# Experts: the order of SyncE's store of X, the unit in which the routing weights are turned, and ACT's order at entry

## The reference, cut to what matters

```
xn = layernorm(x) * gamma + beta
abel_out = gelu(xn @ abel_w + abel_b)
logits = xn @ gate_w + gate_b                       # 8 experts
topw, topi = top_k(logits, 2); topw = softmax(topw)
w_dense = sum(one_hot(topi) * topw)                  # token x expert weights
h = gelu(xn @ ew1[e] + eb1[e])                       # every expert, on every token
eo = h @ ew2[e] + eb2[e]
moe = sum_e eo * w_dense[e], then three rotations
gate = sigmoid(concat(abel_out, moe) @ gc_w + gc_b)
x = x + 0.5 * (layernorm(x) + abel_out * (1 - gate) + moe * gate)
```

## Time and profile before

| | |
|---|---|
| median of 3 runs | 1024.81 us (1024.4 to 1026.99) |
| the profiled execution | 1027.39 us, of which the span of its instructions is 1025.7 us |
| mean granted TensorE clock, as a share of full speed | 0.931 |
| busy: PE, DVE, ACT, POOL | 84%, 71%, 63%, 59% of the span |
| stage 4 | from about 307 to 544 us of the span |
| stage 6 | from about 775 us to the end |

### The profile page before, as it was taken

The page is one execution under the profiler, slowest core; times in us unless marked ns, Lnnn a source line. Parts: engine busy times, 40 slices in busy tenths (PEclk is TensorE's granted clock), DMA queues, the critical chain, the costliest instruction groups (busy, mean ns, idle before and its releaser), DMA issues.

```text
span 1025.7 us, 14084 instructions
## 1 busy us (share of the span) xinstructions
PE 859.0 (84%) x3830; PEld 459.1 (45%) x3830; DVE 725.1 (71%) x1549; ACT 648.1 (63%) x1169; POOL 604.2 (59%) x611
## 2 busy tenths in 40 slices
PE   7889777678966999999994888888866998889997
PEld 6744333373423444444442455555534444444443
DVE  6945479964555788888872477777784878877774
ACT  3177499957745888888763343333324878777874
POOL 2164776566468776666673354444457757555664
PEclk9989799969986999999997899999986999999999
DMA  8000000000002222222200000000002221122220
GB/s 209 11 2 0 0 1 1 0 1 2 0 0 83 83 84 83 82 83 82 82 1 1 0 1 1 1 1 1 1 0 83 84 73 46 68 93 93 93 93 21
DMA packets 27406, 42.10 MB, mean 41 GB/s; under 512 B 5320, under 2 KB 19036, under 8 KB 27356
## 3 DMA queue, kind: packets, MB, share of 16 engines
q1 hardware_dynamic: 27356, 41.52, 12.2%
HBM read 39.15 MB, written 2.36 MB: 40 GB/s over the span
## 4 chain that ended last, share of the span: by engine, by line
PE 28%; issue 26%; POOL 21%; DVE 16%; ACT 5%; DMA 1%; SPq 1%; POOLq 1%; DVEq 0%; ACTq 0%
POOL arena L786 10%; PE bank L1476 5%; PE bank L1478 5%; PE bank L1477 5%; POOL arena L806 5%; POOL arena L750 4%; PE bank L1700 3%; DVE arena L1317 1%; ACT bank L993 1%; DVE stats L1166 1%; PE bank L1670 1%; PE bank L1707 1%; PE bank L1559 1%; DMA arena<-wrows 1%; ACT arena L989 1%
## 5 line engine op out<-in xcount | busy, mean ns | idle before, releaser
L786 POOL TENSOR_TENSOR arena<-arena 128x512 f16<-128x512 f32 x256 | 294.5, 1162 | 141.7 <-ACT arena L989 139.9
L1317 DVE TENSOR_TENSOR arena<-bank,arena 128x512 f32<-128x512 f32 x256 | 173.6, 685 | 89.7 <-ACT bank L993 48.5
L989 ACT ACTIVATE arena<-arena 128x512 f16<-128x512 f32 x256 | 161.3, 630 | 81.5 <-DVE arena L1317 81.0
L993 ACT ACTIVATE bank<-bank,eb 128x512 f32<-128x512 f32 x256 | 167.1, 657 | 18.1 <-PE bank L1478 17.2
L1477 PE MATMUL bank<-arena,ew1hi 128*128 128x512 f16 x256 | 101.6, 397 | 0.0
L813 POOL TENSOR_TENSOR arena<-arena 128x512 f32<-128x512 f32 (+1 forms) x24 | 32.7, 1372 | 117.0 <-DVE arena L1440 89.8
L1476 PE MATMUL bank<-arena,ew1hi 128*128 128x512 f16 x256 | 101.2, 395 | 0.0
L1478 PE MATMUL bank<-arena,ew1lo 128*128 128x512 f16 x256 | 101.1, 395 | 0.0
L1476 PE MATMUL bank<-arena,ew2hi 128*128 128x512 f16 x256 | 97.1, 379 | 0.8 <-POOL arena L786 0.6
L1477 PE MATMUL bank<-arena,ew2hi 128*128 128x512 f16 x256 | 97.0, 379 | 0.0
L1478 PE MATMUL bank<-arena,ew2lo 128*128 128x512 f16 x256 | 97.0, 379 | 0.0
(11 more groups left out here) (273 smaller groups left out, 1879.5 us busy)
## 6 DMA issues: line engine op xcount, KB each, us to landing
arena<-wrows SPq DMA_DIRECT2D x64, 512.0 KB, 5.6
X<-in_L_attn_x_dram SPq DMA_DIRECT2D x8, 256.0 KB, 4.3
out_dram<-X SPq DMA_DIRECT2D x8, 256.0 KB, 2.3
arena<-in_L_ffn_ew_dram SPq DMA_DIRECT2D x2, 512.0 KB, 6.5
arena<-in_L_ffn_ew_dram SPq DMA_DIRECT2D x1, 1024.0 KB
wrows<-arena SPq DMA_DIRECT2D x16, 16.0 KB
arena<-in_L_ffn_gens_dram SPq DMA_DIRECT2D x1, 192.0 KB, 2.6
arena<-in_L_ffn_w_gate_dram SPq DMA_DIRECT2D x1, 192.0 KB, 2.8
```

The costliest lines, as they stand in the source:

```text
L786: pool.tensor_tensor(mo.hlo[:, u % 8, :], mo.hw[:, u % 4, :], mo.hhi[:, u % 8, :], ALU.subtract).then_inc(S.hlo, 1)
L989: A(mo.hhi[:, u % 8, :], mo.hw[:, u % 4, :], ACT.Copy).then_inc(S.hhi, 1)
L993: A(bank[MM1_BANK[u]][:, :], bank[MM1_BANK[u]][:, :], ACT.Gelu, scale=1.0 / WS, bias=eb1[:, u:u + 1]).then_inc(S.gelu, 1)
L1317: TT(mo.hw[:, u % 4, :], bank[MM1_BANK[u]][:, :], mo.wB[:, p, u // EB, :], ALU.mult)\
```

## The change

On SP, in stage 6, the store of chunk c is moved behind the routes of chunk c+2 (it was ahead of them). On PE the turning of the routing weights moves from unit 9 to unit 10, and the abel matmuls from unit 11 to unit 12, where they stand behind the turning of `mo.r`. DVE's copy of the turned weights moves from unit 9, behind `hw(9)`, to unit 10, behind `hw(10)` and the two gate operations. In the second pass of a stage (`mid` without `lag`) ACT copies the turned chunk in unit 1, behind the GELU of unit 1 and ahead of `high(0)`; in the other passes nothing changes for it. `mo.wT` gets a place in the arena behind stage 5's buffers, and its zeroing moves to the start of stage 3, with a wait for the setup matmuls that read the memory that it now takes. PE also waits for the previous copy of the weights before it writes new logits into bank 7.

```diff
@@ arena @@
-        a.used = max(a.used, TM_WORDS)
-        mo.wT = a.take([2, CH])
...
         fl.bdm = a.take([2, CH])
+        a.used = max(a.used, TM_WORDS)
+        mo.wT = a.take([2, CH])
@@ sync @@
+            def store(c):
+                sp.wait_ge(MO.x, c + (NCH + 1 + CREDIT))
+                sp.dma_start(out_parts[:, :, c:c + 1, :], X4[:, :, c:c + 1, :]).then_inc(stored, 16)
...
             for c in range(NCH):
                 if c + 1 < NCH:
                     routes(NCH + c + 1)
-                sp.wait_ge(MO.x, c + (NCH + 1 + CREDIT))
-                sp.dma_start(out_parts[:, :, c:c + 1, :], X4[:, :, c:c + 1, :]).then_inc(stored, 16)
+                if c:
+                    store(c - 1)
+            store(NCH - 1)
@@ gpsimd, ahead @@
                 if number == 2:
                     bias_parts()
+                if number == 3:
+                    pool.wait_ge(S0.small2, 1)
                     pool.memset(mo.wT, 0.0)
@@ scalar, experts @@
+                    def copies(i):
+                        act.wait_ge(S.tr, i + 2)
+                        A(mo.xn, bank[6][:, :], ACT.Copy).then_inc(S.xn, 1)
+                        A(mo.xhi[:, 1 - p, :], bank[6][:, :], ACT.Copy).then_inc(S.xhi, 1)
                     for u in range(NU):
                         if mid:
...
+                            if u == 1 and not lag:
+                                copies(i)
                             if u:
                                 high(i, u - 1)
-                        if lead and u == 2:
-                            act.wait_ge(S.tr, i + 2)
-                            A(mo.xn, bank[6][:, :], ACT.Copy).then_inc(S.xn, 1)
-                            A(mo.xhi[:, 1 - p, :], bank[6][:, :], ACT.Copy).then_inc(S.xhi, 1)
+                        if lead and u == 2 and (lag or not mid):
+                            copies(i)
@@ vector, experts @@
-                        if lead and u == 9:
+                        if lead and u == 10:
                             dve.wait_ge(S.wpT, i + 2)
                             after(dve, S.wd, 16 * i)
                             dve.tensor_copy(mo.wT[0:E, n, :], bank[7][0:E, :]).then_inc(S.wT, 1)
@@ tensor, experts @@
                         if lead and u == 3:
                             pe.wait_ge(S.xn, i + 2)
+                            if mid:
+                                pe.wait_ge(S.wT, i + 1)
...
-                        if lead and u == 9:
+                        if lead and u == 10:
                             pe.wait_ge(S.wpair, i + 2)
...
-                        if mid and u == 11:
+                        if mid and u == 12:
                             if lead:
                                 pe.wait_ge(S.wT, i + 2)
                             three(bank[7][:, :], abhi[:, :], ablo[:, :], mo.xhi[:, p, :], mo.xlo[:, p, :])
```

## The result

The changed kernel takes 1015.63 us (median of 4 runs, 1014.93 to 1016.21) where the kernel before took 1025.9 (4 runs, 1024.4 to 1029.71): a ratio of 0.9886, with a 95% interval of 0.9865 to 0.9907 (the quotient of the two medians alone is 0.990, which lies in it). Of 1024.81 us that is 11.7 us less (9.5 to 13.8). The forecast was 14.5 us less. The profiled execution has a span of 1014.5 us against 1025.7, 11.2 us less.

What follows compares the result with a forecast made beforehand. Waits were taken to decide, with PE fullest: the late weights' broadcast in stage 6 and a 27.13 us loop through PE and DVE. -13.4 + 4.1 - 5.2 = -14.5 us, from 1024.81 to 1010.3 us; range 1005 to 1016.

Steps and rivals of the forecast that it cites:

- the store's order: Stage 6: with the store of X moved behind the routes, its excess over stage 4 goes: -13.4 us.
- turning in unit 10, abel behind `mo.r`: Twelve full passes each 0.27 us longer, PE waiting for `mo.r`: +3.2 us; passes without `lead` +0.9 us; sum +4.1 us.
- ACT's order at entry: Second pass of both stages: `hw(4)` comes 2.6 us sooner; -2.6 us an entry, -5.2 us for two.
- B: Rival: the broadcast of the weights stays late; if half of the 13.4 us stays, 1017 us; chance 0.12.
- D: Rival: the store's move does nothing, since the waits only went to PE's L1682: 1024 us; chance 0.03.
- A: Rival: the move to unit 10 pays, `mo.r` isn't late; -15.6 in place of +3.2 us, 991.5 us; chance 0.10.
- C: Rival: the wait before `mo.r` lowers PE's clock in twelve passes, 1.8 us each, 22 us: 1032 us; chance 0.05.

Runs made afterwards that it cites:

- store alone: The kernel before with only SP's new store order, everything else as before: 1013.96 us, ratio 0.9857.
- entry back: The changed kernel with ACT's old order at entry (copies in unit 2, behind `high(1)`, in every pass): 1019.74 us, ratio 0.9917.
- The POOL experiment: Abel in unit 11, DVE's copy behind `hw(9)`, plus POOL's fourth norm part at stage 4's entry moved behind unit 3's low part: 1007.87 us, ratio 0.9807.

## Why the prediction was nearly right, point by point

| term | forecast | by the stages' lengths | and with the last 5 us as before |
|---|---|---|---|
| the store's order (store alone against before) | -13.4 | -13.2 | -14.1 |
| turning in unit 10, abel behind `mo.r` (entry back against store alone) | +4.1 | +4.4 | +5.7 |
| ACT's order at entry (after against entry back) | -5.2 | -2.8 | -3.9 |
| the clock in the last 5 us | 0 | | +0.7 |
| ahead of and between the stages | 0 | +0.4 | +0.4 |
| sum | -14.5 | -11.2 | -11.2 |

The first column was worked out from the trace of before, the others from single traces, each good to about 1 us at best (the stretch between the stages, which no experiment touches, varied by 3.1 us). Other orders of taking the parts give other prices: they don't simply add. The sum came 3.3 us short, since the gain at entry was overrated and the stages' new length underrated. The rest was near, with some luck in the second row: 4.1 was 3.2 us for full passes, too little, and 0.9 us that came only in small part.

**The store.** The step from the earlier trace rows held in mechanism and size. Comparing the six passes of stage 6 with the same six of stage 4 gave 13.4 us where the list of waits offered 25.4. Rivals B and D are out: no wait for a broadcast but at the entries. One support of the estimate doesn't hold. The prediction set 1.90 us for the weights' store beside the figure of the Trainium skill (DMA: Bandwidth & Descriptors, Anatomy of one DMA), 2.0 us and the bytes, and called it agreement. That section gives the figure for DMAs that GpSimd issues, and here SP issues them. And the 1.90 us have X's store 0.56 us ahead of them; in stage 4, with nothing ahead, the same store took 1.46 to 1.48 us up to the issue of the broadcasts. The measurement decides, and the sum did not use the figure.

**The turning.** Also held: a wait of 1.43 us (forecast 1.5) ahead of L1691, released by the gate's second operation, and 0.38 us (0.4 to 0.5) at the weights. A full pass grew by 0.45 in place of 0.27 us, since the turning of `mo.r` behind this wait takes 0.59 us to the next matmul (421.16 to 421.75), not the 0.43 us that it takes where PE doesn't wait for it: 12 x 0.45 = 5.4 us in place of 3.2. The 0.9 us for the two passes without `lead` came only in part (+0.2 us in stage 4, 23.52 to 23.71 from abel to abel), for there PE has no wait at `mo.r`. At stage 6's entry, with ACT's new order, the later turning even saved something, as the version with the turning back in unit 9 fell to the lower clock there (29.65 in place of 26.70 us, once).

**ACT's entry: the step that failed in part.** "`hw(4)` follows GELU 4 and L1327 at about 325.7 ..., 2.6 us sooner" was right for stage 6 (hw(0) to hw(4) 4.24 us) and wrong for stage 4, where it came 1.0 us sooner. The prediction had read that POOL is at its norms until 325.74 and let only PE wait for it. But `hw(4)` writes a buffer that the low part of unit 0 must have read, so DVE waits for POOL too, 1.50 us by its row. The POOL experiment confirmed it: norm away, `hw(0)` to `hw(4)` 4.24 us in stage 4 as well. In stage 6 the gain did arrive, 2.8 us up to the third store of weights, part of it by the clock, which the prediction had at nothing.

**The rivals.** A (no wait for `mo.r`, 991.5 us) didn't come: the wait is there at the place worked out. But the turning in unit 10 is worth having once the copy, the abel and `mo.r` are placed for it: that version takes 1001 us. C (the clock) didn't come for this change, its twelve passes all at 1.00, with a wait of 1.43 us in each. But it was nearer than its 0.05 said: with 0.6 us more of wait at about the same place (the version with `mo.r` in 13 alone) it came behind five of twelve waits, at 1.67 us for a pass against the 1.8 us that I had taken from the earlier trace rows. The Trainium skill (TensorE: Matmul & The Clock Gate, What's actually happening) has the clock follow how busy the array has been of late; the traces agree so far as each fall named here stood behind a wait (3.75, 2.99, 2.46, 2.02, 2.01, 1.57 us), and show equal waits with and without one.

## What to carry to other kernels

When a step is moved past a point where its engine waits for another, what stood in the shadow of that wait now follows it: list what was hidden there before you move it, and move the hidden work first. The same move to unit 10 made full passes 0.45 us longer (abel and copy behind the gate), 0.13 us shorter (copy ahead of it, abel in 11) or up to 0.6 us shorter (copy ahead, abel in 12 and `mo.r` in 13), by what moved along. Before a gain that was "given back" is put down to an engine, compare the clock in both traces: POOL's moved norm was worth 2.2 us by the third store where it spared a fall, and 0.3 and 0.5 us where the fall only came later. For a wait that an edit removes, go through every condition of the next instruction, the buffer it writes too, not only its inputs. And a store that nobody waits for costs its queue's owner the wait ahead of it: look on each queue for a wait that stands before work already ready.

## What the runs showed of the hardware

- The granted clock is not a function of one wait. Two equal passes in a row, with the same wait of 2.02 us, had 0.94 and 1.00 for the pass (a fall behind 5 of 12 such waits in one kernel, 8 of 12 in another). Waits of 2.45 or 2.46 us at stage 6's entry had a fall in one kernel of nine, of 2.99 to 3.01 us for POOL in two of three, and of 1.57 us at the end of a stage in some kernels. Waits of 1.43 us in twelve passes left it at 1.00.
- A fall cost 1.67 us a time in a full pass, so 0.6 us more of wait ahead of the abel (2.02 in place of 1.43) could bring a further loss of nearly three times that.
- PE's turning of `mo.r`, four 128x128 fp32 blocks, takes 0.43 us up to the next matmul in a full queue and 0.59 us behind a wait of 1.43 us. It isn't every turning: that of the weights (form 128*8 in its row) takes 0.43 or 0.44 us behind waits of 0.38, 1.66 and 2.45 us as well. Why the two differ is not shown.
- The 16 KB store of the weights took 1.46 to 1.48 us up to the issue of the broadcasts that wait for it, in all of stage 4, before and after. With the 256 KB store of X issued 0.56 us ahead it took 1.90 us.
